# One PSUM operand for the small feed-forward operations of VectorE, the squares on ScalarE, a bias on GpSimd

## What is computed

```python
s = attention(xn)            # 32 heads, 8 key/value heads, rope, causal softmax, output product
thought = LN(xn)[:, -1, :] @ agg_w + agg_b                  # 4 rows of 1024
for _ in range(4):
    t = gelu(LN(thought) @ d1_w + d1_b)                     # 4 x 4096
    thought = thought + (t @ d2_w + d2_b)                   # 4 x 1024
broadcast = thought @ bc_w + bc_b
g = silu(LN(xn + sigmoid(xn @ gate_w + gate_b) * broadcast))
out = x + s * g
```

## Time and profile before

| | us |
|---|---|
| median of three runs | 2617.49 (2617.3 to 2618.78) |
| profiled execution, its own time | 2619.42 |
| its span, first to last instruction | 2617.7 |

### The profile page before, as it was taken

The page is one execution under the profiler, slowest core; times in us unless marked ns, Lnnn a source line. Parts: engine busy times, 40 slices in busy tenths (PEclk is TensorE's granted clock), DMA queues, the critical chain, the costliest instruction groups (busy, mean ns, idle before and its releaser), DMA issues. The chain is left out here.

```text
span 2617.7 us, 43494 instructions
## 1 busy us (share of the span) xinstructions
PE 2496.9 (95%) x14156; PEld 1683.3 (64%) x14156; DVE 1731.1 (66%) x3496; ACT 986.0 (38%) x1649; POOL 1374.9 (53%) x640
## 2 busy tenths in 40 slices
PE   5999999997999999999999999999579999999998
PEld 4888888883555545554555545554268888888886
DVE  6444555544777787777777777776267777777777
ACT  2111111111666656665666646666321111111111
POOL 1111111113899989998999988999511111111111
PEclk9999999997999999999999999999789999999999
DMA  6544444547666556555556646664566666666666
GB/s 241 185 164 158 158 162 163 182 154 221 193 199 189 172 163 206 168 174 186 175 166 191 201 135 192 198 194 141 159 158 120 123 119 123 120 121 120 120 120 120
DMA packets 228081, 428.90 MB, mean 164 GB/s; under 512 B 16900, under 2 KB 99844, under 8 KB 227992
## 3 DMA queue, kind: packets, MB, share of 16 engines
q1 hardware_dynamic: 154600, 375.85, 43.5%
q0 software_dynamic: 73392, 51.91, 13.3%
HBM read 313.67 MB, written 113.51 MB: 163 GB/s over the span
## 5 line engine op out<-in xcount | busy, mean ns | idle before, releaser
L925 DVE CUSTOM_DVE_ANT_0 bcast<-mxp,mask_q 128x128 f32<-128x128 f32 (+7 forms) x1024 | 726.1, 753 | 306.9 <-PE mxp L1029 172.5
L843 ACT ACTIVATE pr<-stp 128x512 f32<-128x512 f32 x1152 | 649.4, 595 | 488.1 <-PE stp L1038 365.5
L1038 PE MATMUL stp<-qs,ks 97*128 97x512 f32 x1152 | 478.1, 453 | 3.4 <-ACT pr L843 2.9
L463 PE MATMUL eo<-xt,w 128*128 128x512 f32 x1920 | 449.9, 393 | 3.6 <-DVE xt L380 3.6
L794 POOL TENSOR_TENSOR acc<-acc,pr 128x2048 f32<-128x2048 f32 x96 | 440.7, 4590 | 4.4 <-POOL acc L794 3.8
L463 PEld LDWEIGHTS eo<-xt,w 128*128 128x128 f32 x1920 | 359.1, 189 | 77.8 <-issue 4.0
L1397 PE MATMUL gp<-g,xa 128*128 128x512 f32 x1536 | 355.3, 390 | 17.5 <-DVE g L1336 17.5
L1397 PE MATMUL op<-o,ya 128*128 128x512 f32 x1536 | 355.9, 391 | 13.1 <-DVE ya L1340 13.1
L1038 PEld LDWEIGHTS stp<-qs,ks 97*128 97x128 f32 x1152 | 208.8, 189 | 247.7 <-ACT pr L843 116.6
L1397 PEld LDWEIGHTS gp<-g,xa 128*128 128x128 f32 x1536 | 289.6, 189 | 78.5 <-DMA xa<-xt_scratch 18.3
L1397 PEld LDWEIGHTS op<-o,ya 128*128 128x128 f32 x1536 | 290.1, 189 | 73.9 <-DVE ya L1340 13.5
(11 more groups left out here) (147 smaller groups left out, 3060.6 us busy)
## 6 DMA issues: line engine op xcount, KB each, us to landing
wch<-in_d_w SPq DMA_DIRECT2D x132, 1024.0 KB, 9.7
qs<-q_scratch SPq DMA_DIRECT2D x192, 256.0 KB, 7.7
xa<-xt_scratch POOLq DMA_DIRECT2D x66, 512.0 KB, 6.4
xt_scratch<-xt SPq DMA_DIRECT2D x16, 2048.0 KB, 14.4
q_scratch<-r SPq DMA_DIRECT2D x64, 512.0 KB, 3.6
yr<-y_scratch POOLq DMA_DIRECT2D x33, 512.0 KB, 5.8
xs<-in_x SPq DMA_DIRECT2D x33, 512.0 KB, 5.5
y_scratch<-ys SPq DMA_DIRECT2D x65, 256.0 KB, 2.1
```

The lines of the kernel that those rows point to most:

```text
L463: last = nc.tensor.matmul(out, lhs[a](k), rhs[c](k), start=(k == 0 and (a, c) == (0, 0)), stop=(k == KT - 1 and (a, c) == (1, 0)))
L843: nc.scalar.activation(pr[half][:, :, at:at + P], stp[u % 2][:].rearrange("p (h t) -> p h t", h=REP), ACT.Exp, scale=SCALE).then_inc(act_d ...
L925: last = nc.vector.tensor_tensor_reduce(out=bcast[:, k % 2, hh * step:hh * step + w], in0=mxp[k % 2][:, hh * step + c0:hh * step + c0 + w] ...
L1038: last = nc.tensor.matmul(bank, ks[par][:, j * P:(j + 1) * P], qs[par][:, i // 4, :, (i % 4) * P:(i % 4 + 1) * P], start=True, stop=i != j)
```

## The change

Every `chunk_out` becomes two additions that each take one operand from `trp` in PSUM and one from SBUF: first half plus bias (or plus `th`) into `fr`, then second half plus `fr` into the target. They are chained by `link`. The signals `hp_done` and `t_done` become instructions of their own. The d2 bias is added to `th` by GpSimd in each `ln_pool`, ahead of the d2 sums of that step, in place of L1001 and L995. The first `chunk_out`, ahead of the turns, takes the same form and replaces L960. The squares are made by ScalarE behind the exp of unit 21, and VectorE's sum of them moves from slot 20 to a new entry `lq` at the end of slot 22.

```diff
-22: rc 0, mx 10
+22: rc 0, mx 10, lq
@@ ln_pool (GpSimd)
                 nc.gpsimd.tensor_tensor(rs[:], ve[:], mhalf[:], ALU.pow).then_inc(ln_rs, 1)
+                nc.gpsimd.tensor_tensor(th, th, fvec[:, 3, :].unsqueeze(2).to_broadcast([P, KT, B]), ALU.add)
                 pool.wait_ge(ln_rs, 3 * k + 1)
@@ ScalarE
+            def squares(tu):
+                act.wait_ge(tr_free, tu + 2)
+                nc.scalar.activation(sq[:], cen[:], ACT.Square).then_inc(sq_done, 1)
+
             max_rows(0, 1)
             copy_burst(2)
+            squares(5)
...
+                        elif e[0] == "lc" and "l0" in use:
+                            squares(tb + use["l0"])
@@ VectorE
-            def layernorm_centre(tu, base):
+            def layernorm_centre(tu):
                 dve.wait_ge(tr_full, tu + 1)
                 nc.vector.tensor_tensor(cen[:], th, rows(trp[:, 0:B]), ALU.subtract).then_inc(tr_free, 1)
-                dve.wait_ge(tr_free, tu + 2)
-                link(nc.vector.tensor_tensor(sq[:], cen[:], cen[:], ALU.mult), base)
+
+            def layernorm_squares(k):
+                dve.wait_ge(sq_done, k + 1)
                 nc.vector.tensor_reduce(s2[:], sq[:].rearrange("p k r -> p r k"), AX.X, ALU.add).then_inc(ln_sum, 1)
...
-            def chunk_out(tu, base):
+            def four(ap):
+                return ap.rearrange("p (n c) r -> p n c r", n=2)
+
+            def chunk_out(tu, into, base, addend):
                 dve.wait_ge(tr_full, tu + 1)
                 v = trp[:].rearrange("p (c n k r) -> p n c r k", c=4, n=2, k=2)
-                for nb in range(2):
-                    last = nc.vector.tensor_reduce(fr[:, 4 * nb:4 * nb + 4, :], v[:, nb, :, 0:B, :], AX.X, ALU.add)
-                last.then_inc(tr_free, 1)
-                dve.wait_ge(tr_free, tu + 2)
+                link(nc.vector.tensor_tensor(four(fr[:]), v[:, :, :, 0:B, 0], four(addend), ALU.add), base)
+                return nc.vector.tensor_tensor(four(into), v[:, :, :, 0:B, 1], four(fr[:]), ALU.add)
...
                         elif e[0] == "ft":
-                            chunk_out(tb + use["ft"], base)
+                            tu = tb + use["ft"]
                             if par == 0:
                                 dve.wait_ge(b1_in, (it + 1) * 16)
-                                nc.vector.tensor_tensor(hpre[:], fr[:], bc(b1c[:], B), ALU.add).then_inc(hp_done, 1)
+                                chunk_out(tu, hpre[:], base, bc(b1c[:], B)).then_inc(tr_free, 1)
+                                dve.wait_ge(tr_free, tu + 2)
+                                dve.sem_inc(hp_done, 1)
                             else:
-                                link(nc.vector.tensor_tensor(th, th, fr[:], ALU.add), base)
+                                chunk_out(tu, th, base, th).then_inc(tr_free, 1)
+                                dve.wait_ge(tr_free, tu + 2)
                                 if left == 1:
-                                    nc.vector.tensor_tensor(th, th, bc(fvec[:, 3, :], B), ALU.add).then_inc(t_done, 1)
+                                    dve.sem_inc(t_done, 1)
...
                         elif e[0] == "ls" and "l0" in use:
-                            link(nc.vector.tensor_tensor(th, th, bc(fvec[:, 3, :], B), ALU.add), base)
                             layernorm_sum()
                         elif e[0] == "lc" and "l0" in use:
-                            layernorm_centre(tb + use["l0"], base)
+                            layernorm_centre(tb + use["l0"])
+                        elif e[0] == "lq" and "l1" in use:
+                            layernorm_squares(s + 1)
```

More of the change, by code:

```diff
@@ L589, in attention_phase @@
         ln_sum, ln_rs = sem("a_ln_sum"), sem("a_ln_rs")
+        sq_done = sem("a_sq")
         link_s = sem("a_link")
@@ L957, in _ @@
                 elif step == 2:
-                    chunk_out(4, 0)
                     dve.wait_ge(c_in, 16 * 12)
-                    link(nc.vector.tensor_tensor(th, fr[:], bc(fvec[:, 0, :], B), ALU.add), 0)
+                    chunk_out(4, th, 0, bc(fvec[:, 0, :], B)).then_inc(tr_free, 1)
+                    dve.wait_ge(tr_free, 6)
                     layernorm_sum()
                 elif step == 3:
-                    layernorm_centre(5, 0)
+                    layernorm_centre(5)
+                    layernorm_squares(0)
                 elif step == 4:
@@ L1203, in _ @@
                 last.then_inc(pick_done, 1)
-LINKS_TURN = 1
-LINKS_STEP = 2
+LINKS_TURN = 2
+LINKS_STEP = 0
 def output_phase(nc, x, woT, gate_w, gate_b, out_g, out_b, xt_d, y_d, mhalf, bcast, out):
```

## The result

The changed kernel takes 2599.23 us (median of four runs, 2597.34 to 2599.78), the kernel before, run beside it, 2618.14: a ratio of 0.9926 [0.9909, 0.9943]. It is 0.7% faster, but 13 us slower than forecast and outside the range of 2577 to 2598. The profiled execution took 2599.45 us, its span 2597.7.

A forecast was written before the change was run, and what follows sets the result against it. TensorE was taken to set the attention phase's pace, with GpSimd close behind. Gains of 7.8 us (odd chunk ends) and 23.5 (layer norm turns) sum to 31.3: 2617.49 - 31.3 = 2586 us, likeliest range 2577 to 2598.

The forecast's parts named there:

- Odd chunk ends: Attention stretches from odd to even chunk ends: VectorE is back some 1.1 us sooner, TensorE gains 12 x 0.65 = 7.8 us.
- The slope of 0.65 us: Plain attention turns: 1.1 us more of VectorE in odd turns costs TensorE only 37.31 - 36.66 = 0.65 us.
- Turns with a layer norm: Three attention stretches holding a layer norm: 140.22 us in all before, 38.9 us each after, clock at 1.00.
- The wait for the centring: Layer norm turns: TensorE's product `ss 0` waits 1.4 us for the bank that VectorE's centring frees, three times.
- the 23.5 us: Gain of the three layer norm stretches, from taking the bias and squares with two SBUF operands off VectorE.
- a two-operand read waits: VectorE: a read of two SBUF operands waits for the running GpSimd instruction's end; one with a PSUM operand does not.
- GpSimd's bias at nothing: GpSimd's layer norm part: some 2.2 us late, hidden in its waits for TensorE; no loss, at most 6.6 us.
- TensorE's wait for maxima: Sign of being right: TensorE's wait at L1025 for VectorE's row maxima falls from 16.2 to a few us.
- The square's table loads: Rival, chance 0.11: ScalarE's squares cost two table loads each, 41.5 us for a layer norm turn, time 2594.
- idle odd turns: Rival, chance 0.10: odd turns gain nothing, only the layer norm turns' 23.5 us remain, time 2594.
- PSUM operands: Rival, chance 0.02: chunk-end additions wait reading `trp` while TensorE writes other banks; slower, 2636 at 1.25 us each.
- every operation wait that begins beside a GpSimd addition: Rival, chance 0.03: anything VectorE starts beside a GpSimd addition waits, so the new operations wait too, time 2617.

The follow-up runs named there:

- 1392: The changed kernel with one more instruction on VectorE ahead of its loops, so the third turns loop begins at instruction 1392: 2584.89 us.
- 1393: The changed kernel with 2 more instructions on VectorE ahead of its loops, so the third turns loop begins at instruction 1393: 2587.94 us.
- 1399: The changed kernel with 8 more instructions (semaphore increments) on VectorE ahead of its loops: 2585.72 us, ratio 0.9871.
- 1391: Third loop's place in the changed kernel (2599.23 us), kept with 8 instructions more behind VectorE's loops (2599.3 us) or ahead of ScalarE's (2601.55 us).

## Why the prediction was wrong, step by step

- **Odd chunk ends, "I take all of it: 12 x 0.65 = 7.8 us".** This is where the result left the forecast: the twelve stretches grew by 5.7 us. Ten of them behaved (36.6), two held a fetch stall. The step priced VectorE's instructions by their durations and had no term for where its code lies, and the sum had none either. The missing term is 14.4 us; 2599.45 - 14.4 = 2585.1, against 2588.1 for the profiled execution. That the place of VectorE's loops makes the stall is shown by five kernels: free at 1392, 1393 and 1399, stalled at 1391 with the program changed elsewhere in two ways. The packets of q14 from 1306.2 to 1480 go with it: 11 in each stalled kernel, none or one in the free kernels at 1392, 1393 and 1399. No trace of before could show the price, and the range wasn't widened for it.
- **The slope of 0.65 us** was right: 447.73 to 439.25 without the stall.
- **Turns with a layer norm, 38.9 us each.** Measured 38.45, 38.45 and 38.95. The wait for the centring was 1.1 us where 1.4 was forecast, the clock stayed at 1.00, and no table load came.
- **Why these turns gain** was wrong, and the total hid it. The prediction gave the 23.5 us to the moves of the bias and the squares. With the new chunk end alone the stretches fell from 46.7 to 38.8. The earlier trace rows held the hint: the bias began 0.20 us behind L794. I read that as "a two-operand read waits", and didn't ask whether it would still begin there once the chunk end was 1.1 us shorter. That the kernel without the stall takes 2585.7 us where I forecast 2586 is thus in part luck: the size was right, the credit was not.
- **GpSimd's bias at nothing**: right. Its waits for the partition sums were 47.2 us, 32.3 in the kernel with 8 more instructions, against 49.5: less slack, none of it missed, as the plain stretches behind (37.1, 36.65 and 36.65) are as long as before. The sum in that step was off (38.1 + 0.2 - 2.6 is 35.7, not 35.5), and nothing hung on it.
- **TensorE's wait for maxima** at L1025 (16.2 us) has no row at L1040 any more. In its place stand the two waits behind the fetch stalls at L1046.
- **Rivals.** The square's table loads (2594) and idle odd turns (2594) are excluded by the rows above; that their 2594 lies near the result means nothing. PSUM operands don't wait: 0.186 and 0.192 us. Nor does every operation wait that begins beside a GpSimd addition: the centring's 0.18 us above.

## What to carry to other kernels

A small operation with two SBUF operands beside a busy GpSimd is priced by when it begins: look up the start of the GpSimd instruction next to it in the timeline, redo that for the shifted schedule, and try another place in the order before another engine. Parts of a change that remove the same wait don't add up: time each alone and all together. And when the number of instructions changes ahead of a hardware loop, look first for idle time put down to "issue" behind its back jumps; one idle instruction was worth some 14 us here, beside 33 for the change.

## What the runs showed that I had not expected

- A back jump of VectorE can cost 7.2 to 7.6 us of its time, and with the lower granted clock behind it 6.5 to 8.1 us of the kernel's. It came in all three kernels with the loop at 1391 and not in the one with the loop at 1392 (one run); each pair came with 9 or 10 packets more in the instruction queue q14 (49 against 39 or 40).
- The same addition of 32 elements took 0.19, 2.86 and 4.34 us, by its start against GpSimd's.
- With a stall of 2.86 us on VectorE a layer norm turn got about 5 us longer (14.7 us for three turns, 2601.49 against 2586.76): the mean product stood behind it in TensorE's order, and the granted clock fell from 1.00 to 0.92. A part of it may belong to the later place of the sum.
